# Routing the first batch's tokens inside the second batch's attention, and what the stage after attention then holds

## The chip, the core and the metric

One core of a Trainium2 chip (trn2). TensorE (PE) multiplies matrices, VectorE (DVE), ScalarE (ACT) and GpSimd (POOL) work on tiles, SyncE (SP) issues most DMAs. The metric is device time in microseconds of the one core.

## The reference, cut to what matters

Two sequences of 1024 tokens with 256 features go through one transformer layer: grouped attention (16 query heads, 4 key-value heads of 128, causal, rotary positions), layernorm, a mixture of experts, layernorm.

```
q = rope(x @ Wq.T); k = rope(x @ Wk.T); v = x @ Wv.T
x = layernorm(x + softmax(causal(q k^T / sqrt(128))) v @ Wo.T)
logits = x @ gate_w.T                      # (2048, 64)
topk_w, topk_ids = top_k(softmax(logits), 6);  topk_w /= sum(topk_w)
routed = sum over the 6 experts of  w * (silu(g) * u) @ w_down.T
shared = (silu(x @ sg.T) * (x @ su.T)) @ ws_down.T
x = layernorm(x + routed + shared)
```

## The kernel before, in words

There are three blocks of engine programs, one after the other: attention, routing (with the shared experts), experts. All engines meet at the end of a block.

**Attention** is software-pipelined in 4 rounds (k = 0 to 3) of 64 steps. A round takes two key-value heads of one batch, so batch 0 is done in rounds 0 and 1, batch 1 in rounds 2 and 3. A step is one tile of 128 queries of one head against its 1 to 8 tiles of 128 keys: of each 32 steps the first 16 have 1 to 4 key tiles (here the short half), the last 16 have 5 to 8 (the long half). The order on every engine is written out by the step number n: TensorE in step n forms the scores of n, transposes the probabilities of n-2, sums the output of the pair (n-4)/2, and does one fill of the projection bank proj_ps, if FILLS names one. Every product is three products of upper and lower parts (hi and lo, fp32r). FILLS: O (output projection of a pair) at steps 4m and 4m+1, Q at 4m+2, and at 4m+3 in turn T, K, V and nothing. K and Q are turned by the rotary tables: ScalarE copies the bank (taken), GpSimd multiplies by the cosine in two operations of 64 partitions that swap the halves (L347, L349), VectorE by the sine (turn_sin, L490), GpSimd adds (L353) and forms the lower part (L333). V comes as T, a product of 512 columns that is transposed later by 4 transposes (fill V, L585). VectorE takes the row maximum (neg_max, L508), the lower parts of probabilities (pt_lo, L468) and outputs (o_lo, L476) and adds the projected output to resid (L501). A fill waits (bank_free) until the one before it is taken out of the bank. Meanwhile SP writes SKIP rows into the buffer of expert rows in DRAM (rows_dram), 32 DMAs from 114 partitions, 8 rows each.

**Routing** takes all 16 tiles of 128 tokens together: statistics, square root on ScalarE, norm (L803), transposes to xt (L910), logits (L919), MAX8 and indices, masks of the six chosen experts (L816 to L821), counts and places by products with triangular and one matrices (L927 to L933), slot numbers (product, slots, slots_int, L854 to L856), then owner, triples (L858 to L865), the table of which expert each block of 256 rows has. ScalarE copies each token's row six times into rows (L768). GpSimd sends 96 indirect DMAs of 128 rows into rows_dram (L752). The shared experts run on TensorE (L942 gate-up, L956 and L957 down), 16 units in order, each of which needs a product by VectorE (hide, L875, L876) two units before it.

**Experts** walks over the blocks in triples; SP reads each block's expert from the table and loads rows (x_in) and weights.

Of the kernel before, what the change touches and what calls it, by code (L numbers as in the profile page):

```python
# [30 lines left out]
P = 128  # L31
B, S, H = 2, 1024, 256
T = B * S
# [20 lines left out]
LIST_BLOCKS = MAX_BLOCKS + 3  # L54
ROWS = LIST_BLOCKS * BLK
EMPTY_ROWS = 8
# [25 lines left out]
               key=lambda use: FILLS[use[0]][use[1]])  # L82
SPLIT_X = [-20, -4]
SPLIT_W = [-16, 16]
SPLIT_WO = [2, 34]

# [55 lines left out]

def runs(i, per, first, last):


    return i is not None and not (first and i < per) and not (last and i >= per)


def now(k, per, n):


    return (k + 1) * per + n

# [9 lines left out]
def attention(nc, dram, resid, consts):  # L163
    with ExitStack() as ctx:
# [24 lines left out]
        probs = sb("probs", [P, 4, S])  # L189
# [3 lines left out]
        ident = consts["ident"]  # L193

# [6 lines left out]
        x_in, w_in, wo_in, empty_out = sem("x_in"), sem("w_in"), sem("wo_in"), sem("empty_out")  # L201
# [5 lines left out]
        v_turning = sb("v_turning", [P, HALF])  # L207
# [7 lines left out]

        block = ctx.enter_context(nc.Block())
# [4 lines left out]
        def w_cols(kind, i):  # L221

            head = {"K": GROUP, "T": GROUP + 1}.get(kind, i % GROUP)
            return slice(head * HD, (head + 1) * HD)
# [15 lines left out]

        def lower_parts(eng, ops, k, n, first, last):

            i = at(SPLIT_X, n)
            if runs(i, SPLITS, first, last):
                cols = slice(i % 2 * HALF, (i % 2 + 1) * HALF)
                eng.wait_ge(x_hi_made, now(k, SPLITS, i + 1))
# [11 lines left out]
        def _(sp):  # L258
# [3 lines left out]
            def body(k, first, last):  # L262
                def batch_of(r):
                    return r % ROUNDS // (NKV // KV_ROUND)

# [4 lines left out]
                for n in range(FIRST, FIRST + STEPS):  # L270
                    i = at(SPLIT_X, n)
                    if runs(i, SPLITS, first, last):
                        sp.wait_ge(x_split, now(k, SPLITS, i))
                        sp.dma_start(x_raw[:], dram["xT"][bass.ds(batch_of(k + i // SPLITS), 1), i % 2]
                                     .rearrange("o p k t -> (o p) k t")).then_inc(x_in, 16)
# [10 lines left out]
                    if first and n == FIRST + STEPS - 1:  # L286
                        sp.dma_start(resid[:], dram["x"].rearrange("(i p) c -> p i c", p=P)).then_inc(resid_in, 16)
                        sp.wait_ge(consts_made, 2)
                    if not first and n % 8 == 0:
# [159 lines left out]
        def _(dve):  # L449
# [9 lines left out]
            def body(k, first, last):  # L459
# [60 lines left out]
                if first:  # L520
                    dve.wait_ge(resid_in, 16)
# [945 lines left out]
```

## Time and profile before

| | us |
|---|---|
| median of 3 runs | 1422.31 (1422.07 to 1423.52) |
| the profiled execution | 1425.77 |
| its span, first to last instruction | 1424.0 |
| attention | 0 to 884.1 |
| routing | 884.1 to 1077.2 |
| experts | 1077.2 to 1424.0 |

The profile records when each instruction ran on its engine and what it waited for. A busy TensorE is not TensorE at its peak. All times are from the start of the span.

### The profile page before, as it was taken

How to read it: one execution, taken by the hardware profiler on the slowest of the kernel's cores; microseconds unless marked ns; L12 is line 12 of the kernel's file. 1: busy time of each engine (PE TensorE's matmuls, PEld its weight loads, DVE VectorE, ACT ScalarE, POOL GpSimd, SP SyncE). 2: the span in 40 equal slices, each digit the busy share in tenths (PEclk: the TensorE clock that was granted, in tenths of full speed). 3: DMA queues.
4: the chain of work that ended last, by engine and by line, in shares of the span. 5: the costliest groups of instructions: out<-in, count | busy, mean ns of one | idle time of the engine just before them, and what ended most of it. 6: DMA issues, size and time to landing. Idle time of an engine off the chain costs nothing. (4 is left out here: it accounts for less than half of the span.)

```text
span 1424.0 us, 27954 instructions
## 1 busy us (share of the span) xinstructions
PE 1254.1 (88%) x8732; PEld 1117.1 (78%) x8732; DVE 991.5 (70%) x2012; ACT 846.5 (59%) x1875; POOL 809.8 (57%) x798
## 2 busy tenths in 40 slices
PE   3899999999999999999999997539925999999966
PEld 2789899899899899899899897536615999999954
DVE  2677677677677677777776777572204999999956
ACT  2666666566666566666665664622204989899932
POOL 4754754654754654754654630037774888888840
PEclk9999999999999999999999999559966999999979
DMA  6320040120040120140400001014225888888868
GB/s 224 116 76 1 11 153 23 57 76 1 21 151 15 57 76 1 27 150 11 122 1 2 1 1 34 1 49 104 104 101 172 263 260 262 257 263 263 267 204 269
DMA packets 100293, 151.29 MB, mean 106 GB/s; under 512 B 10410, under 2 KB 73038, under 8 KB 100196
## 3 DMA queue, kind: packets, MB, share of 16 engines
q1 hardware_dynamic: 89156, 124.75, 29.0%
q0 software_dynamic: 11040, 25.30, 5.3%
q8 instruction: 54, 0.88, 0.3%
q14 instruction: 43, 0.35, 0.1%
HBM read 92.51 MB, written 62.46 MB: 109 GB/s over the span
## 5 line engine op out<-in xcount | busy, mean ns | idle before, releaser
L508 DVE TENSOR_REDUCE neg_max<-scores 128x1 f32<-128x256 f32 (+7 forms) x256 | 192.6, 752 | 178.3 <-PE scores L611 178.1
L418 ACT ACTIVATE pt_hi<-pt 128x512 fp32r<-128x512 f32 (+3 forms) x384 | 174.8, 490 | 204.8 <-PE pt L620 201.7
L468 DVE TENSOR_TENSOR pt_lo<-pt,pt_hi 128x512 fp32r<-128x512 f32 (+3 forms) x384 | 200.8, 551 | 23.5 <-ACT pt_hi L418 21.6
L391 ACT ACTIVATE probs<-scores,neg_max 128x256 f32<-128x256 f32 (+7 forms) x256 | 190.1, 743 | 21.9 <-DVE neg_max L508 21.8
L539 PE MATMUL o_ps<-pt_hi,v_hi 128*128 128x256 f32 (+1 forms) x640 | 193.4, 302 | 4.9 <-DVE o_lo L476 4.8
L347 POOL TENSOR_TENSOR turned<-taken,cos 64x512 f32<-64x512 f32 x80 | 105.6, 1320 | 152.7 <-ACT taken L401 147.5
L540 PE MATMUL o_ps<-pt_lo,v_hi 128*128 128x256 f32 (+1 forms) x640 | 179.5, 281 | 0.0
L541 PE MATMUL o_ps<-pt_hi,v_lo 128*128 128x256 f32 (+1 forms) x640 | 179.1, 280 | 0.0
L620 PE MATMUL pt<-ident,probs 128*128 128x128 f32 x1152 | 168.2, 273 | 0.0
L1106 POOL DMA_INDIRECT results_dram<-y_sb,dest x134 | 145.2, 1083 | 32.8 <-issue 25.9
L611 PE MATMUL scores<-k_hi,q_lo 128*128 128x512 f32 (+4 forms) x384 | 151.5, 395 | 0.0
L333 POOL TENSOR_TENSOR q_lo<-turned,q_hi 128x512 fp32r<-128x512 f32 x64 | 82.6, 1291 | 113.9 <-ACT q_hi L428 113.9
L353 POOL TENSOR_TENSOR turned<-turned,turn_sin 128x512 f32<-128x512 f32 x80 | 103.8, 1298 | 72.7 <-DVE turn_sin L490 71.2
L752 POOL DMA_INDIRECT rows_dram<-rows,slots_int x96 | 94.2, 982 | 86.0 <-issue 86.0
L620 PEld LDWEIGHTS pt<-ident,probs 128*128 128x128 f32 x1152 | 134.9, 141 | 5.0
L606 PE MATMUL scores<-k_hi,q_hi 128*128 128x512 f32 (+4 forms) x384 | 132.1, 344 | 2.7 <-POOL q_lo L333 2.7
L607 PE MATMUL scores<-k_lo,q_hi 128*128 128x512 f32 (+4 forms) x384 | 131.1, 341 | 0.0
L539 PEld LDWEIGHTS o_ps<-pt_hi,v_hi 128*128 128x128 f32 x640 | 121.1, 189 | 10.2 <-issue 7.4
L540 PEld LDWEIGHTS o_ps<-pt_lo,v_hi 128*128 128x128 f32 x640 | 121.9, 191 | 0.0
L541 PEld LDWEIGHTS o_ps<-pt_hi,v_lo 128*128 128x128 f32 x640 | 121.2, 189 | 0.0
L501 DVE SCALAR_TENSOR_TENSOR resid<-proj_ps,row_inv,resid 128x256 f32<-128x256 f32 x256 | 110.7, 473 | 7.5 <-PE proj_ps L541 7.5
L349 POOL TENSOR_TENSOR turned<-taken,cos 64x512 f32<-64x512 f32 x80 | 105.8, 1323 | 6.3
(186 smaller groups left out, 3619.0 us busy)
## 6 DMA issues: line engine op xcount, KB each, us to landing
rows_dram<-empty SPq DMA_DIRECT2D x32, 919.1 KB
up_raw<-in_up SPq DMA_DIRECT2D x69, 368.0 KB, 3.9
x_in<-rows_dram SPq DMA_DIRECT2D x68, 258.0 KB, 3.5
parts<-results_dram SPq DMA_DIRECT2D x16, 768.0 KB, 9.8
down_raw<-in_down SPq DMA_DIRECT2D x69, 128.0 KB
down_raw<-in_down_tail SPq DMA_DIRECT2D x69, 112.0 KB
w_raw<-in_w SPq DMA_DIRECT2D x8, 768.0 KB, 9.1
x_raw<-in_xT SPq DMA_DIRECT2D x8, 512.0 KB, 5.0
```

What stands on the lines that cost most here:

```text
L391: nc.scalar.activation(probs[:, m % 4, 0:w], scores_ps[m % 2][:, score_cols(m)], ACT.Exp, bias=neg_max[:, m % 4:m % 4 + 1], accum_out=row_ ...
L418: nc.scalar.activation(pt_hi[m // 2 % 2][:, a:z, P * (m % 2):P * (m % 2) + P], pt_ps[c % 2][:, 0:P * (z - a)].rearrange("p (k q) -> p k q" ...
L468: nc.vector.tensor_tensor(pt_lo[m // 2 % 2][part], pt_ps[c % 2][:, 0:P * (z - a)].rearrange("p (k q) -> p k q", q=P), pt_hi[m // 2 % 2][pa ...
L508: nc.vector.tensor_reduce(neg_max[:, n % 4:n % 4 + 1], scores_ps[n % 2][:, score_cols(n)], AX.X, ALU.max, negate=True).then_inc(max_made, 1)
L539: nc.tensor.matmul(out, lh, rh, start=first, stop=False)
L540: nc.tensor.matmul(out, lh, rl, start=False, stop=False)
L541: return nc.tensor.matmul(out, ll, rh, start=False, stop=last)
L606: nc.tensor.matmul(out, q_hi[b][qt], k_hi[u][:, keys], start=True, stop=False)
L607: nc.tensor.matmul(out, q_hi[b][qt], k_lo[u][:, keys], start=False, stop=False)
L611: mm = nc.tensor.matmul(out, q_lo[b][qt], k_hi[u][:, keys], start=False, stop=True)
L620: mm = nc.tensor.transpose(pt_ps[c % 2][:, (t - a) * P:(t - a + 1) * P], probs[:, m % 4, t * P:(t + 1) * P], ident[:])
L1106: pool.indirect_dma_start(out=dram["results"], out_offset=bass.IndirectOffsetOnAxis(ap=dest[buf][:, s:s + 1], axis=0), in_=y_sb[buf][:, s, ...
```

## The change

The eight tiles of batch 0 (EARLY) are routed during the attention of batch 1, in two groups of four tiles (GT = 4, GROUPS = 4). Their VectorE operations are dealt over steps by the table EARLY_DVE, their transposes, logits and places are made by TensorE in the projection bank at steps 4m+3 (EARLY_TURN, EARLY_LOGITS, EARLY_PLACE), and their 48 sends go out two steps apart, in the end one step apart (EARLY_FILL), through a ring of four row buffers. For slots to be known before all counts are, each expert gets an area of 2048 rows in rows_dram; the block table then holds a row block for each block too, and SP reads it in the expert loop. The routing block does the other eight tiles (LATE); the counts move behind the slots, the shared experts' loops are written out. To make room in attention: V of rounds 2 and 3 is formed directly (no T), the rotary swap moves from GpSimd's cosine to VectorE's sine, x is split only once for each batch, probs has 2 buffers for 4, loads are issued 12 steps ahead. The clearing of rows_dram becomes 64 DMAs from 65 partitions, 32 rows each, one every four steps and never more than about 8 steps ahead of TensorE.

```diff
-LIST_BLOCKS = MAX_BLOCKS + 3
-ROWS = LIST_BLOCKS * BLK
-EMPTY_ROWS = 8
+CAP = T
+AREAS = E + 1
+ROWS = AREAS * CAP
+EMPTY_ROWS = 32
+EMPTY_DMAS = CAP // EMPTY_ROWS
+GT = 4
+GROUPS = TILES // GT
+EARLY = BT
+LATE = TILES - EARLY
+LOAD_AHEAD = 12
+EMPTY_EVERY = 4
+TURNED_V_ROUNDS = 2
+EARLY_DVE = {(1, 55): [(0, "stats", 0), (0, "stats", 1)], (1, 57): [(0, "stats", 2)], (1, 58): [(0, "stats", 3)],
...
+             (2, 31): [(0, "shift", 0), (1, "inverse", 0)], (2, 35): [(0, "weigh", 0)], (2, 39): [(0, "weigh", 1)],
+             (2, 43): [(0, "slot", 0)], (2, 47): [(0, "slot", 1)], (2, 50): [(0, "slot", 2)],
...
+             (3, 54): [(1, "slot", 8)], (3, 55): [(1, "slot", 9), (1, "slot", 10)], (3, 57): [(1, "slot", 11)]}
+EARLY_DEVIATION = {(1, 60): 0, (2, 20): 1}
+EARLY_EXP = {(2, 32): 0, (3, 28): 1}
+EARLY_TURN = {(2, 3): (0, 0), (2, 15): (0, 1), (2, 63): (1, 0), (3, 3): (1, 1)}
+EARLY_LOGITS = {(2, 19): 0, (3, 15): 1}
+EARLY_PLACE = {(2, 31): 0, (3, 31): 1}
+RING_ROWS = 4
+SENDS = EARLY * WAYS
+EARLY_FILL = {step: f for f, step in enumerate([2 * STEPS + 49 + 2 * f for f in range(SENDS // 2)]
+                                               + [3 * STEPS + 41 + 2 * f for f in range(GT)]
+                                               + [3 * STEPS + 48 + f for f in range(SENDS // 2 - GT)])}
...
@@ attention, SP
-                    if not first and n % 8 == 0:
-                        sp.dma_start(dram["empty"][bass.ds(k * 8 + (n // 8 - 1), 1)].rearrange("o p r c -> (o p) r c"),
-                                     empty[0:LIST_BLOCKS, :].unsqueeze(1).broadcast_to([LIST_BLOCKS, EMPTY_ROWS, ROW])).then_inc(empty_out, 16)
+                    if not first and step % EMPTY_EVERY == 0:
+                        c = (k * STEPS + step) // EMPTY_EVERY - FIRST // EMPTY_EVERY - 1
+                        sp.wait_ge(scored, now(k, STEPS, step - 8))
+                        sp.dma_start(dram["empty"][c], empty[0:AREAS, :].unsqueeze(1).broadcast_to([AREAS, EMPTY_ROWS, ROW])).then_inc(empty_out[c * GROUPS // EMPTY_DMAS], 16)
@@ attention, GpSimd
+            def send(f):
+                g, t, way = fill_of(f)
+                pool.wait_ge(rows_filled, f + 1)
+                pool.wait_ge(slots_made, g * TOPK + way + 1)
+                pool.wait_ge(empty_out[g], 16 * EMPTY_DMAS // GROUPS)
+                pool.indirect_dma_start(
+                    out=dram["rows"], out_offset=bass.IndirectOffsetOnAxis(ap=slots_int[:, t, way:way + 1], axis=0),
+                    in_=rows[:, f % RING_ROWS, :], in_offset=None, bounds_check=ROWS - 1,
+                    oob_is_err=False).then_inc(rows_sent[f % RING_ROWS], 16)
-                        nc.gpsimd.tensor_tensor(turned[r % 2][0:64], taken[r % 2][64:128], cos[64:128, pos], ALU.mult).then_inc(cos_made, 1)
-                        pool.wait_ge(cos_made, 2 * now(k, len(ROPES), r) + 1)
-                        nc.gpsimd.tensor_tensor(turned[r % 2][64:128], taken[r % 2][0:64], cos[0:64, pos], ALU.mult).then_inc(cos_made, 1)
+                        nc.gpsimd.tensor_tensor(turned[r % 2][:], taken[r % 2][:], cos[:, pos], ALU.mult).then_inc(cos_made, 1)
+                    if k * STEPS + n - 1 in EARLY_FILL:
+                        send(EARLY_FILL[k * STEPS + n - 1])
@@ attention, ScalarE, at the end of a step
+                    if k * STEPS + n in EARLY_FILL:
+                        f = EARLY_FILL[k * STEPS + n]
+                        g, t, way = fill_of(f)
+                        act.wait_ge(weights_made, g + 1)
+                        act.wait_ge(normed, GT * (g + 1))
+                        if f >= RING_ROWS:
+                            act.wait_ge(rows_sent[f % RING_ROWS], 16 * (f // RING_ROWS))
+                        nc.scalar.activation(rows[:, f % RING_ROWS, 0:H], resid[:, t, :], ACT.Copy)
+                        nc.scalar.activation(rows[:, f % RING_ROWS, H:ROW], goes_with[:, t, way, :],
+                                             ACT.Copy).then_inc(rows_filled, 1)
@@ attention, VectorE
+                nc.vector.tensor_tensor(turn_sin[r % 2][0:64], taken[r % 2][64:128], sin[64:128, pos], ALU.mult)
+                nc.vector.tensor_tensor(turn_sin[r % 2][64:128], taken[r % 2][0:64], sin[0:64, pos],
+                                        ALU.mult).then_inc(sin_made, 1)
...
+                    turn = fill_at(n - 2)
+                    if turn and turn[0] == "Q" and runs(turn[1], per("Q"), first, last):
+                        turn_by_sine(k, *turn)
...
+                    if turn and turn[0] == "K" and runs(turn[1], per("K"), first, last):
+                        turn_by_sine(k, *turn)
                     if runs(n, STEPS, first, last):
                         dve.wait_ge(scored, now(k, STEPS, n + 1))
                         nc.vector.tensor_reduce(neg_max[:, n % 4:n % 4 + 1], scores_ps[n % 2][:, score_cols(n)],
                                                 AX.X, ALU.max, negate=True).then_inc(max_made, 1)
+                    route(k, n)
@@ attention, TensorE
+                    if kind == "V":
+                        for t in range(4):
+                            tok = slice((4 * half(kind, i) + t) * P, (4 * half(kind, i) + t + 1) * P)
+                            for c in range(HK):
+                                mm = products(proj_ps[:, t * HD:(t + 1) * HD], (x_hi[:, c, tok], x_lo[:, c, tok]),
+                                              (w_hi[u][:, c, w_cols(kind, i)], w_lo[u][:, c, w_cols(kind, i)]), c == 0, c == HK - 1)
@@ routing, TensorE
             pe.wait_ge(shared_in, 48)
+            pe.wait_ge(xt_made, TILES // 2)
+            pe.wait_ge(mask_made, 1)
             gate_up(0, 0)
             gate_up(0, 1)
-            pe.wait_ge(slots_made, TOPK)
-            with pe.Fori(0, UNITS // 4 - 1) as q:
+            for q in range(UNITS // 4 - 1):
@@ experts, SP
-                sp.dma_start(x_in[buf][:], row_blocks[bass.ds(n, 1)].rearrange("o p s c -> (o p) s c")).then_inc(rows_in[buf], 16)
+                r = sp.value_load(table[0:1, bass.ds(P + n, 1)], min_val=0, max_val=ROWS // BLK - 1)
+                sp.dma_start(x_in[buf][:], row_blocks[bass.ds(r, 1)].rearrange("o p s c -> (o p) s c")).then_inc(rows_in[buf], 16)
```

## Rows read from the trace of the kernel before

**Rows 1.** Windows by stage: length, busy us (instructions) of each engine, PE clock, DMA share, GB/s.
```profile
34.00:884.10 850.10, 826.48 (x5860) 742.45 (x5860) 614.94 (x1182) 528.17 (x1230) 461.08 (x334) 1.00 0.16 49
884.10:1077.20 193.10, 111.20 (x568) 82.34 (x568) 70.08 (x191) 47.57 (x73) 96.83 (x107) 0.73 0.24 72
1077.20:1372.00 294.80, 270.62 (x2148) 259.57 (x2148) 266.18 (x541) 252.83 (x541) 238.74 (x341) 0.96 0.82 250
```

**Rows 2.** Timeline of VectorE in the routing stage: start, us, instruction, idle before.
```profile
891.44 5.26 DVE L803 TENSOR_SCALAR resid<-resid,moments,inv_dev 128x256 f32<-128x256 f32 x16
...
911.57 2.20 DVE L809 MAX8 top<-logits_ps 128x8 f32<-128x64 f32 x16 [14.88 <-PE logits_ps L919]
...
928.07 1.23 DVE L824 TENSOR_TENSOR shifted<-logits_ps,top 128x1024 f32<-128x1024 f32 x1 [0.15 <-DVE mask L821]
...
939.06 1.22 DVE L854 TENSOR_TENSOR product<-chosen,slot_of 128x1024 f32<-128x1024 bf16 x1
...
954.75 0.25 DVE L858 TENSOR_SCALAR started<-started,block_id 128x64 f32<-128x64 f32 x1
...
956.04 0.15 DVE L865 TENSOR_SCALAR triples_int<-triples_int 128x1 int32<-128x1 int32 x1
...
1041.22 0.69 DVE L884 TENSOR_TENSOR resid<-places_ps,resid 128x512 f32<-128x512 f32 x1 [4.33 <-PE places_ps L957]
```

**Rows 3.** Timeline of ScalarE in the routing stage.
```profile
910.18 17.95 ACT L768 ACTIVATE rows<-resid 128x1536 f32<-128x1536 f32 x13
928.15 1.28 ACT L772 ACT_TABLE_LOAD   x1
```

**Rows 4.** Timeline of GpSimd: the first two of 96 sends, and the last.
```profile
942.78 1.18 POOL L752 DMA_INDIRECT rows_dram<-rows,slots_int  x1 [57.06 <-issue]
944.26 0.98 POOL L752 DMA_INDIRECT rows_dram<-rows,slots_int  x1 [0.30 <-issue]
...
1064.98 0.98 POOL L752 DMA_INDIRECT rows_dram<-rows,slots_int  x1 [0.30 <-issue]
```

**Rows 5.** Instructions of the routing block's end (ns min/median/max; first start).
```profile
L654 POOLq DRAIN  x1: 7910/7910/7910, 1067.7 to 1067.7; - x1
```

**Rows 6.** Timeline of TensorE at the shared experts' start.
```profile
956.22 3.75 PE L942 MATMUL logits_ps<-xt,shared_up 128*128 128x256 f32 x8 [20.90 <-DVEq L868]
...
964.70 1.99 PE L942 MATMUL logits_ps<-xt,shared_up 128*128 x8 [0.56 <-DVE shared_hidden L876]
```

**Rows 7.** TensorE's waits from 50 to 880 us: total us, times, longest.
```profile
PE proj_ps L539 <- DVE v_lo L514: 10.4, 8, 1.3
PE proj_ps L539 <- DVE resid L501: 5.2, 8, 0.7
PE o_ps L539 <- DVE o_lo L476: 3.6, 16, 0.3
```

**Rows 8.** Timeline of TensorE in attention: products of 512 and of 128 columns.
```profile
521.38 0.40 PE L540 MATMUL proj_ps<-x_lo,w_hi 128*128 128x512 f32 x1
521.62 0.39 PE L541 MATMUL proj_ps<-x_hi,w_lo 128*128 128x512 f32 x1
...
525.81 0.28 PE L540 MATMUL o_ps<-pt_lo,v_hi 128*128 128x128 f32 x1
525.92 0.27 PE L541 MATMUL o_ps<-pt_hi,v_lo 128*128 128x128 f32 x1
```

**Rows 9.** The sine turn's line: ns min/median/max, first and last start.
```profile
L490 DVE TENSOR_TENSOR turn_sin<-taken,sin x80: 681/1022/1545, 20.3 to 843.4; 128x512 f32<-128x512 f32 x80
```

**Rows 10.** The same as rows 5, for the attention block's end.
```profile
L164 POOLq DRAIN  x1: 1409/1409/1409, 849.5 to 849.5; - x1
```

**Rows 11.** Windows of 10 us in attention, with and without clearing (columns as rows 1).
```profile
410.00:420.00 10.00, 10.00 (x72) 8.99 (x71) 6.57 (x11) 5.94 (x13) 3.72 (x3) 1.00 0.41 126
720.00:730.00 10.00, 10.00 (x77) 9.43 (x76) 8.44 (x16) 6.93 (x15) 3.42 (x4) 1.00 0.00 1
```

**Rows 12.** SP's own waits from 1100 to 1370 us.
```profile
SPq L1059 <- DVE down_lo L1269: 68.3, 63, 1.9
```

More of the change, by code:

```diff
@@ new lines, in early_at, with fill_of, early_bank @@
+def early_at(schedule, k, n):
+    for way_in in ((k, n), (k - 1, n + STEPS), (k + 1, n - STEPS)):
+        if way_in in schedule:
+            return schedule[way_in]
+    return None
+def fill_of(f):
+    g, way, t = f // (GT * WAYS), f // GT % WAYS, f % GT
+    return g, GT * g + t, way
+def early_bank(k, n):
+    for kind, uses in (("turn", EARLY_TURN), ("logits", EARLY_LOGITS), ("place", EARLY_PLACE)):
+        if early_at(uses, k, n) is not None:
+            return kind, early_at(uses, k, n)
+    return None
@@ L262, in body @@
             def body(k, first, last):
-                def batch_of(r):
-                    return r % ROUNDS // (NKV // KV_ROUND)
                 def kv_at(i):
                     return (k + i // SPLITS) % (NKV // KV_ROUND) * KV_ROUND + i % SPLITS
[L270 to L275, printed above, removed]
+                for step in range(FIRST, FIRST + STEPS):
+                    n = step + LOAD_AHEAD
+                    i = x_part(k, n, first, last)
+                    if i is not None:
+                        sp.wait_ge(x_split, SPLITS + i)
+                        sp.dma_start(x_raw[:], dram["xT"][i // SPLITS, i % 2]).then_inc(x_in, 16)
                     i = at(SPLIT_W, n)
@@ L544, in bank_free @@
                 def bank_free(n):
-                    for before in range(n - 1, 0, -1):
-                        use = fill_at(before)
-                        if use and (before < FIRST or runs(use[1], per(use[0]), first, last)):
+                    for earlier in range(n - 1, 0, -1):
+                        use = early_bank(k, earlier)
+                        if use:
+                            break
+                        use = fill_at(earlier)
+                        if use and use[0] == "T" and not turned_v(k, use[1]):
+                            continue
+                        if use and (earlier < FIRST or runs(use[1], per(use[0]), first, last)):
                             break
@@ L639, in body @@
                     use = fill_at(n)
-                    if use and runs(use[1], per(use[0]), first, last):
+                    if use and runs(use[1], per(use[0]), first, last) and (use[0] != "T" or turned_v(k, use[1])):
                         fill(n, *use)
+                    turn = early_at(EARLY_TURN, k, n)
+                    if turn is not None:
+                        bank_free(n)
+                        g, h = turn
+                        pe.wait_ge(normed, GT * g + 2 * h + 2)
+                        for t in range(2):
+                            for c in range(HK):
+                                mm = nc.tensor.transpose(proj_ps[:, (t * HK + c) * P:(t * HK + c + 1) * P],
+                                                         resid[:, GT * g + 2 * h + t, c * P:(c + 1) * P], ident[:])
+                        mm.then_inc(turned_x, 1)
@@ L774, in _ @@
             act.sem_inc(silu_made, 3)
-            with act.Fori(0, UNITS // 4) as q:
+            for q in range(UNITS // 4):
                 for u in range(4):
@@ L928, in _ @@
             mm.then_inc(places_made, 1)
-            for i in range(TILES):
+            for i in range(LATE):
                 out = places_ps[:, i * E:(i + 1) * E]
```

499 lines of the change are left out of this document (354 added, 145 removed).

## The prediction

> **What bounds the kernel.** I read the windows by stage first. Attention takes 850 us and TensorE is busy for 826 of them; the stage between attention and the experts takes 193.1 us with TensorE busy 111 and VectorE 70; the expert stage takes 295 us with VectorE and TensorE both above 90% [rows 1]. The 193 us stage is where no engine is full, so I read it engine by engine. VectorE first: layernorm, then a wait for the logits, top-6 and mask until 928.1, slot numbers from 939.1 to 954.8, the block table until 956.2 [rows 2]. ScalarE copies the rows to be sent, 13 tiles in 17.95 us, 1.38 us each, and loads a function table in 1.28 us [rows 3]. GpSimd starts its first send at 942.8; the second starts at 944.3 and the last of 96 at 1065.0, one every 1.284 us [rows 4]. The block then ends on GpSimd: its drain behind the sends lasts 7.9 us, to 1075.6 [rows 5]. TensorE starts the shared experts at 956.2, waits once for VectorE, runs from 964.7 without a gap [rows 6] and its last sum is added by 1041.9 [rows 2]. So the sends are last, 34 us behind the shared experts. From 50 to 880 us TensorE waits for somebody for only 19 us: 10.4 for v_lo, 5.2 for the addition into resid, 3.6 for o_lo [rows 7]. That stage is a full TensorE stream; anything added to it on TensorE is paid in full, and what is added elsewhere is paid where those waits grow.
>
> **The stage after attention, now for 8 of 16 tiles.** Its zero is its start, 884.1. Before, norm starts at 7.3 and the first max at 27.5, 20.1 us for 16 tiles [rows 2]. With half the stats norm starts at 4.3; two tiles must be normed before the first pair is turned (+0.7), and 8 tiles take half of 20.1, so the max starts at about 15.5 to 16. From max to mask was 16.5 us for 16 tiles [rows 2]; half is 8.3, and the two subtractions moved ahead add 0.8: mask at 25. On TensorE 44 mask products follow instead of 152, some 2 us, to 27. ScalarE has three more pairs to copy (to 19.5), then 8 tiles of rows at 1.38 and two exponentials with a table load, 11.0 + 2.1 [rows 3]: to 32.8. That is later than VectorE's weights (30), so the rows are ready at 33.2. Six slots at half of 15.7/6 us [rows 2] take 8.2, to 41.4. The table calculation, 7 operations in 1.44 us before [rows 2], is now some 19 in a row with the count of blocks in it: 4.0, to 45.5.
>
> The sends: the first at 33.2 + 1.4 + 1.1 = 35.7; 47 spacings and 1.2 for the last, 61.6; then landing and the drain of 7.9: 107.
>
> The shared experts: their first two units now run at 27 to 36, but the third needs the first product of VectorE, which is in order behind the table calculation: 46.6 on TensorE. From there to the last addition it took 964.70 to 1041.91, 77.2 us [rows 2, 6]. TensorE is idle for 10 us before; after its idle time before 956.2 the first eight gate-up products took 3.75 us where later ones take 1.99 [rows 6], 1.8 more, with their tail some 2.5, and I add that. End: 46.6 + 79.7 = 126.3, with VectorE's own drain 126.9. This is 20 us behind the sends: **the end moves from GpSimd to TensorE**. The stage ended at 1075.6 - 884.1 = 191.5, so the gain is 64.6 us, not the 84 that the sends alone would give. Unrolling the loop gives nothing: TensorE had no gap in it.
>
> **What attention pays.** (1) V of rounds 2 and 3 is formed directly. A 512-column product is issued 0.24 us after the one before it, a 128-column one after 0.11 [rows 8]. Removed per V: 6 x 0.24 + 4 x 0.1 = 1.8; added 24 x 0.11 = 2.65. Eight times +0.85 = +6.8. In the short half of each 32 steps TensorE stood 1.3 us behind v_lo; the longer product gives VectorE time, so four of these eight waits go: -5.2. (2) K's sine turn moves behind the addition into resid, the addition that TensorE waited for at K steps: -5.2 [rows 7]. (3) The sine turn is split in two operations of 64 partitions, and the swap leaves GpSimd, which has one product where it had two. One turn took 1.02 us in the median and 0.68 at least [rows 9], where GpSimd was quiet; two quiet ones are 1.36. I set this to 0, since GpSimd's second product, which ran beside the turn, is gone; if it isn't hidden it is 0.3 x 80 = 24 us of VectorE, a bound. The Trainium skill (SBUF — State Buffer, Who interferes with whom) says that a VectorE operation with two SBUF inputs contends with GpSimd's SBUF reads; the spread of the turn agrees, and by the rule the split costs less than twice the old mean. (4) TensorE's part of the early routing: four turns of 4 transposes (1.7), logits (2.4, an estimate: half of what 8 tiles of logits took in the stage after attention), 28 mask products (1.5): +5.6. (5) The projection bank: six early uses stand in front of an O fill and are taken late in the next step, by ScalarE or VectorE. By the wait of v_lo about 1 us each, +6; 0 to 12. (6) VectorE's insertions: 51 us for 16 tiles before (70.1 less 19 of shared work [rows 1]), so 26 for 8, about 35 in pieces of 256 columns. VectorE is busy 615 of 850 us [rows 1], so there is room; the price is lateness. Behind the insertion stand pt_lo, o_lo and the resid addition that TensorE needs. In the long half they have over a microsecond of slack, in the short half almost none: 12 short-half insertions at 0.3 to 0.5, the rest little: +6, bounds 0 and 35. (7) ScalarE: 48 fills of two copies, 0.6 us each, 28 us in all. Queued behind is o_hi, for which o_lo and the next output product wait. A dozen lie in the short half, at 0.4; the others at 0.1: +8, bounds 0 and 28. (8) Two square roots force a function table away and back, 4 loads of 1.28 [rows 3]: +3, bounds 0 and 5. (9) 4 of 8 x loads and their splits go, hidden before. The 48 sends on GpSimd take 1.3 us each; it is busy 461 of 850 us [rows 1] and loses 100 us of cosine products, so they are hidden, except at the end. The last fill comes some 6 us before the end of attention at the earliest, its send takes some 3.5 us to land, and then comes the drain: 7.9 us behind sends [rows 5] against 1.4 without them [rows 10]. Attention's block ends at 889 instead of 884: +5, bounds 0 and 9.
> Attention: 6.8 - 5.2 - 5.2 + 5.6 + 6 + 6 + 8 + 3 = +25, and +5 at its end.
>
> **The clearing of rows.** An area of 2048 rows for each expert makes the buffer 65 x 2048 rows of 1032 B, 137 MB; before, 30 MB were cleared. It goes out in 64 transfers of 2.15 MB, one in every 4 steps (13.2 us). The old ones moved 126 GB/s with a busy share of 0.41 of 16 engines [rows 11]: 6.6 engines. The source then had 114 partitions, and 6 is the largest number up to 16 that divides 114; for 65 it is 13. At 20 GB/s for an engine 13 give 260 GB/s, 8.3 us a transfer, and all is hidden; the expert stage shows that 250 GB/s can be had [rows 1]. TensorE was full with 126 GB/s beside it and with 1 [rows 11]. The other bound is 126 GB/s as before: 17 us a transfer. The Trainium skill (DMA: Bandwidth & Descriptors, Why a DMA increments its semaphore by 16 and not by 1) says that a transfer uses the largest number of engines up to 16 that divides the outermost size of both sides; the busy share agrees, and by the rule the clearing is hidden.
>
> **The expert stage.** Block counts are the same. SP reads one more value for each block, under 1 us. SP is queued behind down_lo for 68.3 us in 63 blocks, 1.1 each [rows 12]; the read takes that place. At the start it lies beside GpSimd's zeroing. 0.
>
> **Sum.** The profiled execution took 1425.8 (span 1424.0 and 1.8 around it), 3.5 over the median. 1425.8 - 64.6 + 25 + 5 = 1391; at the median's level 1387.6. I say 1387.
>
> **Rivals.** *A, as summed*, 0.62. *B, attention hides everything* (items 5 to 8 are 0, the rest about 2): 1422 - 65 + 5 = 1363. For it: VectorE idle 28%, ScalarE 38%. Against: short-half waits of rows 7. 0.10. *C, every inserted operation is paid in full*: 35 + 28 + 5.6 + 12 + 5, with the split turn 24: +110 - 65: 1467, slower. It decides from +65 us in attention, half a microsecond in each of 128 steps. 0.07. *D, the clearing keeps 126 GB/s*: 137.4 MB take 1090 us; the block can't end before 1110 to 1120, 230 late, and the total is 1422 - 65 + 230 = 1587. It decides below 162 GB/s for the stretch of 850 us, and turns the sign below some 150. Rows 11 alone speak for it, the share against. 0.08. *E, the shared experts don't wait for the table calculation*, so the sends end the stage at 107 or the shared experts at 113: 14 to 20 us more gain, 1370. 0.05. *F, the change moves work but late routing is held by something else new* (the table's trip, rows), gain near zero: 0.02. The rest, 0.06, is A with an attention cost of 45 to 65.
> Faster 0.82, within 0.2% (what a measurement of this kernel can tell from no change) 0.02, slower 0.16. The range takes in B and A with attention at up to +55: 1360 to 1415.
>
> **What would show it.** The windows: attention 25 to 35 longer, at TensorE near 97% busy; the next stage 127 long instead of 191.5. The chain in it: GpSimd's 48 sends end some 20 us before TensorE's last down product; the third shared unit starts right after the last table operation. GpSimd's drain at attention's end is near 8 us and ends it. The clearing shows a DMA share near 0.8 for 60% of the time. TensorE's waits in the short halves of rounds 2 and 3 name ScalarE and VectorE. Wrong would be: an attention stage over 900 with DMA busy to its end (D), or TensorE's waits above 60 us (C).

## The result and the profile after

The changed kernel takes 1416.9 us in the median of 20 runs (1409.4 to 1421.9), the kernel before 1424.2 (1422.1 to 1426.1, 20 runs): 0.9948 of before, 95% interval 0.9936 to 0.9959. It is faster by 7 us. I had forecast 1387 against the 1422.3 known then, 35 us less; 1416.9 lies 2 us above my range.

The profiled execution of the changed kernel took 1411.4 us with a span of 1409.6. Windows by stage, columns as in [rows 1]:

```profile
34.00:934.00 900.00, 850.49 (x6040) 761.43 (x6040) 693.68 (x1398) 553.23 (x1328) 391.14 (x297) 0.99 0.66 169
934.00:1066.00 132.00, 100.16 (x428) 71.34 (x428) 49.62 (x148) 30.88 (x54) 48.49 (x54) 0.82 0.21 57
1066.00:1372.00 306.00, 278.49 (x2181) 267.14 (x2182) 268.07 (x557) 251.80 (x541) 240.81 (x343) 0.95 0.83 255
```

Against [rows 1] attention ends 50.2 us later (934.3 against 884.1), the routing stage lasts 131.6 us where it lasted 192.0 (-60.4), and what follows 343.7 where it was 347.9 (-4.2). The sum is -14.4 us, the difference of the two spans. That is twice the difference of the medians, because this execution is one of the changed kernel's quickest: in two later profiles of the same kernel (spans 1419.0 and 1418.3) attention took as long within 2 us and the routing stage within 1, but the experts took 350.6 and 350.4 us.

The routing stage came out nearly as forecast. GpSimd's last sends before the stage and the last in it:

```profile
926.02 0.98 POOL L445 DMA_INDIRECT rows_dram<-early_rows,early_slots_int  x1 [0.30 <-issue]
927.30 0.98 POOL L445 DMA_INDIRECT rows_dram<-early_rows,early_slots_int  x1 [0.30 <-issue]
...
968.95 1.01 POOL L1055 DMA_INDIRECT rows_dram<-rows,slots_int  x1 [33.83 <-DVE slots_int L1153]
...
1029.86 0.98 POOL L1055 DMA_INDIRECT rows_dram<-rows,slots_int  x1 [0.30 <-issue]
1065.87 0.53 POOL L1442 MEMSET hidden<- 128x512 f32 x1 [35.03 <-POOLq L957]
```

The first send starts 34.7 us into the stage (forecast 35.7); the last is issued 34 us before VectorE's last addition, and GpSimd then waits 35 us for the block's end. So the end has moved from GpSimd [rows 4, 5] to TensorE. VectorE, at the end of the block table and at the first shared unit, and the last addition:

```profile
979.46 0.15 DVE L1175 CAST triples_int<-triples 128x1 int32<-128x1 f32 x1
979.65 0.15 DVE L1176 TENSOR_SCALAR triples_int<-triples_int 128x1 int32<-128x1 int32 x1
986.00 0.42 DVE L1186 TENSOR_TENSOR shared_hidden<-shared_silu,logits_ps 128x256 f32<-128x256 f32 x1 [6.20 <-ACT shared_silu L1087]
...
1064.29 0.69 DVE L1195 TENSOR_TENSOR resid<-shared_y,resid 128x512 f32<-128x512 f32 x1 [4.33 <-PE shared_y L1271]
```

TensorE in the same stretch:

```profile
979.83 3.75 PE L1256 MATMUL logits_ps<-xt,shared_up 128*128 128x256 f32 x8 [16.89 <-DVEq L1179]
```

TensorE stood for 16.9 us and started its first shared unit when the table was done, 45.6 us into the stage. (A unit is one shared expert's gate and up products for 256 tokens; L1179 is the line where VectorE first releases hidden_made.) The table took from 975.6 to 979.8, 4.2 us (forecast 4.0).

In attention, TensorE's waits from 50 to 880 us, in answer to [rows 7]:

```profile
PE o_ps L789 <- DVE o_lo L728: 20.0, 24, 2.0
PE proj_ps L789 <- DVE v_lo L756: 7.5, 8, 1.5
PE pt L889 <- DVE pt_lo L720: 4.4, 6, 1.1
PE proj_ps L789 <- ACT x_raw L575: 3.6, 4, 2.1
PE proj_ps L789 <- ACT v_turning L583: 3.3, 2, 1.9
PE proj_ps L789 <- DVE resid L748: 2.1, 8, 0.4
PE proj_ps L789 <- DVE base L630: 1.2, 2, 0.7
```

They are 42 us where they were 19, and TensorE's busy time grew by 24, some of it at the lower clock (last section). The wait for o_lo, 3.6 us in 16 places before, is 20.0 us in 24.

From the start of each step's row maximum on VectorE, which stands in every step, one gets the length of 16 steps. The table has attention's 16 groups of 16 in order (two for each half round, the short scores first), each from its first row maximum to that of the next group, the last one to that of step 255:

```
before        40.2 61.4 44.5 61.4 | 44.5 61.4 44.5 61.4 | 44.5 61.4 44.5 61.4 | 44.5 61.4 44.5 52.2
changed       41.6 62.4 46.7 62.4 | 46.7 62.4 46.8 64.0 | 46.2 72.4 47.4 64.8 | 48.6 67.9 48.3 55.0
```

The bars stand between rounds. In the first two rounds the early routing does not yet run, bar a few statistics, and still every group of short scores costs 2.2 us more (the first 1.4) and every group of long ones 1.0. This price repeats to 0.1 us, so it belongs to something in every step. From group 8 on the direct V (below, 0.9 in a long group) and the routing's own price come on top, above all in one group, 72.4.

### The profile page after: what moved, and what is told of

Same layout as the page of the kernel before. It is cut to its first block and busy times, and to the rows that moved or that the text cites. A ratio compares the mean times of both kernels' runs of the same rounds, so it can differ in the third digit from the quotient of the medians.

```text
span 1409.6 us, 28399 instructions
## 1 busy us (share of the span) xinstructions
PE 1264.9 (90%) x8780; PEld 1125.1 (80%) x8780; DVE 1051.0 (75%) x2191; ACT 854.4 (61%) x1956; POOL 694.4 (49%) x718
## 5 line engine op out<-in xcount | busy, mean ns | idle before, releaser
L466 POOL TENSOR_TENSOR turned<-taken,cos 128x512 f32<-128x512 f32 x80 | 104.1, 1301 | 144.9 <-ACT taken L519 144.7
L1422 POOL DMA_INDIRECT results_dram<-y_sb,dest x134 | 148.6, 1109 | 33.7 <-issue 27.3
L789 PE MATMUL proj_ps<-wo_hi,o_hi 128*128 128x256 f32 x256 | 78.0, 305 | 18.9 <-DVE v_lo L756 7.5
L789 PE MATMUL proj_ps<-x_hi,w_hi 128*128 128x512 f32 x176 | 73.6, 418 | 16.5 <-DVE w_lo L356 12.4
## 6 DMA issues: line engine op xcount, KB each, us to landing
wo_raw<-in_wo SPq DMA_DIRECT2D x8, 512.0 KB, 19.4
```

Of the source, the lines that this page charges most:

```text
L789: nc.tensor.matmul(out, lh, rh, start=first, stop=False)
L1422: pool.indirect_dma_start(out=dram["results"], out_offset=bass.IndirectOffsetOnAxis(ap=dest[buf][:, s:s + 1], axis=0), in_=y_sb[buf][:, s, ...
```

## Experiments

Runs beginning with b are the kernel before with one part of the change; those with a are the changed kernel with one part altered. Ratios are against the kernel before on the same chip. This matters: on two of the chips before took 1494 us (last section), on the others 1423 to 1424. The edits are shown shortened, with words for long code.

**The swap of halves alone (b_swap).**

```diff
-  gpsimd: turned[0:64] = taken[64:128] * cos[64:128];  turned[64:128] = taken[0:64] * cos[0:64]
+  gpsimd: turned[:] = taken[:] * cos[:]
-  vector: turn_sin[:] = taken[:] * sin[:]
+  vector: turn_sin[0:64] = taken[64:128] * sin[64:128];  turn_sin[64:128] = taken[0:64] * sin[0:64]
```

> The kernel before with one part of the change: the swap of halves moves from GpSimd's cosine products to VectorE's sine products, so a turn has two sine products of 64 partitions and one cosine product of 128. Theory 1 (half of the 50 us that attention grew by belongs to changes that act in every step, and the split turn is the largest of them): 8 to 20 us slower. Rival (the split is hidden, as I predicted: the 25 us come from elsewhere): within 3 us of before.

1532.9 us against 1494.2, ratio 1.0253 (1.0232 to 1.0273): 38.7 us slower, near twice the most that I expected. VectorE's groups of instructions from 35 to 900 us (count, then busy us and mean ns), first of b_swap:

```profile
L489 DVE TENSOR_TENSOR turn_sin<-taken,sin 64x512 f32<-64x512 f32 x77 | 60.6, 787 | 1.1
L488 DVE TENSOR_TENSOR turn_sin<-taken,sin 64x512 f32<-64x512 f32 x77 | 56.5, 734 | 2.4
```

and of b_order, below, which has the whole product:

```profile
L465 DVE TENSOR_TENSOR turn_sin<-taken,sin 128x512 f32<-128x512 f32 x77 | 75.9, 985 | 0.1
```

117 us where one product takes 76. The quick ones show it best: min and median are 686 and 687 ns for 64 partitions, and 681 is the least for 128 [rows 9]. Half the partitions take VectorE as long as all of them, 0.69 us against 0.68. The Trainium skill (VectorE: DVE Perf Modes, Why `tensor_reduce` can't reduce along partition axis) says that each of the 128 partition lanes is a pipeline of its own; the trace agrees.

Where it is paid, TensorE's waits from 50 to 880 us in b_swap, against [rows 7]:

```profile
PE proj_ps L539 <- DVE resid L501: 21.3, 16, 2.5
PE proj_ps L539 <- DVE v_lo L514: 16.8, 15, 1.7
PE o_ps L539 <- DVE o_lo L474: 2.2, 10, 0.2
```

They are 40.3 us where they were 19.2.

**VectorE's order alone (b_order)**: the row maximum behind v_lo and K's sine product, K's sine product behind the addition into resid.

```diff
-  recip; sine product (K or Q); add into resid; row maximum; v_lo
+  sine product (Q); recip; add into resid; v_lo; sine product (K); row maximum
```

> The kernel before with VectorE's order in a step as in the changed kernel: the row maximum comes behind v_lo and behind K's sine product, and K's sine product behind the addition into resid. I predicted 5.2 us of gain from it. Theory 1: it gains no more than 3 us, or loses up to 5, since the row maximum is now late for the exponential. Rival: the gain of 5 us is there and another part pays more than the trace suggests.

1494.2 us, ratio 1.0005 (0.9994 to 1.0016). Nothing. TensorE's waits from 50 to 880 us:

```profile
PE o_ps L544 <- DVE o_lo L484: 12.5, 24, 1.1
PE proj_ps L544 <- DVE v_lo L512: 5.9, 8, 0.7
PE proj_ps L544 <- DVE resid L504: 1.0, 1, 1.0
```

The wait for resid fell from 5.2 to 1.0 us, nearly as priced, and that for v_lo from 10.4 to 5.9, and the wait for o_lo rose from 3.6 to 12.5. The sum is 19.4 as it was 19.2: the lateness only changed its name.

**Swap and order together (b_order_swap)**, the two diffs above.

> The kernel before with the swap on VectorE and VectorE's order in a step as changed. The swap alone cost 39 us, the order alone 0. Theory (the order is there to let TensorE's two waits, for v_lo and for the addition into resid, come ahead of the longer sine products): together they cost 22 to 28 us, which is what the changed kernel's attention lost in rounds without early routing. Rival (they add up): 36 to 42 us.

1448.8 us against 1423.1, ratio 1.0175 (1.0158 to 1.0192): 25.7 us, inside the 22 to 28. Its groups of steps are 41.8 62.4 47.0 62.4 | 47.0 62.4 47.0 62.4 and so on: the price in the changed kernel's first rounds, to 0.3 us. So the order is worth 13 us once the sine product is split (11 by the length of all steps, 870.4 against 859.6 us; b_swap ran on one of the slower chips), and nothing before. TensorE's waits:

```profile
PE o_ps L544 <- DVE o_lo L484: 19.9, 23, 2.1
PE proj_ps L544 <- DVE v_lo L512: 11.7, 8, 1.5
PE proj_ps L544 <- DVE resid L504: 1.3, 8, 0.2
```

They are 32.9 us, 13.7 more than before. The rest of the price is the clock: seven stretches of about 3.4 us at half clock in attention, where before has none, lose 11.9 us by my estimate (half of their length). Together 25.6, where the steps took 25.7 us longer. In b_swap the same sum is 21.1 of waits and half of nine such stretches, 15.3: 36.4, where the steps took 36.5 longer.

**Two buffers of probabilities (b_probs2)**

```diff
-  probs = sb("probs", [P, 4, S])
+  probs = sb("probs", [P, 2, S])
-  act.wait_ge(transposed, now(k, CHUNKS, chunks_before(m - 3)))
+  act.wait_ge(transposed, now(k, CHUNKS, chunks_before(m - 1)))
```

> The kernel before with two buffers of probabilities in place of four, so ScalarE's exponential of a step waits until TensorE has transposed the probabilities of two steps earlier. Theory: this is the part of the change that nothing in my sum accounts for, 5 to 15 us slower. Rival: the exponential comes later than that transpose anyway; within 2 us of before.

1494.8 us, ratio 1.0001 (0.999 to 1.0013), every group of steps as before. The rival holds.

**The clearing (b_clear64)**

```diff
-  if not first and n % 8 == 0: clear 8 rows of each of 114 blocks
+  if not first and n % 4 == 0: clear 32 rows of each of 65 areas of 2048
```

> The kernel before with the changed kernel's clearing alone: a buffer of 65 times 2048 rows, cleared in 64 transfers of 2.15 MB from 65 partitions, one in every four steps, where 32 transfers of 0.94 MB were. The blocks read the same few rows. Theory: the clearing is hidden, within 3 us of before. Rival 1 (the traffic slows the cores' work or makes the chip grant a lower clock: the clock fell to 0.97 or 0.98 in the first five stretches of the changed kernel's attention): 8 to 15 us slower and the same dips in the granted clock. Rival 2: it is the spread between runs, 12 us wide after and 4 us before, that comes with the clearing.

1493.8 us, ratio 1.0002 (0.9989 to 1.0014). It is hidden, with a DMA share of 0.70 to 0.76 up to 820 us, and the granted clock stays at 1.00 from 140 us on. So the clock's dips are not the traffic's, and neither is the spread (1491.6 to 1498.7, before beside it 1491.4 to 1497.2).

**V formed directly in the last two rounds (b_vdirect)**

```diff
+  if kind == "V" and not turned_v(k, i): 24 products of 128 columns into proj_ps
```

> The kernel before with V of the last two rounds formed directly, and nothing else. I priced it at 6.8 us of TensorE less 5.2 of the waits for v_lo that it covers, +1.6. Theory: 0 to +3 us. Rival: the waits stay and the products are added to them, +6 to +9; or more is covered, -3.

1429.1 us against 1424.3, ratio 1.0028 (1.0018 to 1.0038): +4.8 us, between my theory and the rival. TensorE is busy 7.7 us longer (834.2 against 826.5), where I had priced 6.8; the waits for v_lo fell only from 10.4 to 6.4, where I had priced 5.2, and those for resid and o_lo stayed (5.0 and 3.4 us). The last 1 us stands in gaps too short to be listed as waits. By groups it is 0.9 us in each long one and 0.3 in each short one from group 8 on.

**The changed kernel again (a_again, a_again2)**

> The changed kernel unchanged, as the base for the three beside it and because this chip need not be the one of the first measurement: on the chip of the first four experiments the kernel before took 1494 us instead of 1424, with the shared experts' TensorE waiting for its next instruction while the sends ran. Every theory: if this is a chip of the first kind, 0.995 of before; on one of the second kind the result depends on whether the 48 sends that are left hold the instructions up as 96 did, and could be 0.95 to 1.00.

> The changed kernel once more, as base for the two beside it. On a chip of the first kind 0.995 of before. On one of the second kind (before 1494 us) the two near relatives of it that ran there took 1468 and 1469, so 0.980 to 0.985 is expected: the shared experts' wait for instructions beside the sends shrinks with the number of sends.

1417.7 us, 0.995 (0.9931 to 0.9968), and 1415.6, 0.9931 (0.9914 to 0.9947). The same as at first.

**The swap back on GpSimd where it can be (a_mixed)**: not everywhere. In the kernel before, GpSimd waits for all of its own earlier results before the two swapping products; with sends among them that would be their landings. What that would cost was not measured.

```diff
+  def swaps_on_vector(k, kind, i): return k + i // per(kind) >= ROUNDS - 1
+  where it is false: GpSimd's two cosine products and VectorE's one sine product, as before
-  EARLY_FILL starts at 2 * STEPS + 49
+  EARLY_FILL starts at 2 * STEPS + 57
```

> The changed kernel with the swap of halves back on GpSimd (two cosine products of 64 partitions, one sine product of 128) for the first three rounds' heads; the last round's stay as changed, since GpSimd's sends are under way then, and the first batch's 24 first sends start 8 steps later for the same reason. Theory 1 (the split sine product is most of what attention pays): three quarters of the turns lose 0.5 us of VectorE each, attention gets 20 to 30 us shorter, total 0.975 to 0.985 of before on a chip of the first kind. Rival (the early routing is what costs, the swap is worth 39 us only in the old order): 0 to 8 us.

1408.7 us, ratio 0.9879 (0.985 to 0.9908), 8.9 us less than a_again, where I expected 20 to 30. The groups tell where: 40.2 61.4 44.5 61.4 | 44.5 61.4 44.6 63.5 | 46.3 70.6 47.0 64.7 | 48.6 69.5 51.7 55.0. Until the early routing starts the steps are those of before, 11 us less than changed: the price of the first two rounds is the swap's, and nothing else's. From group 8 to 12 undoing the swap gives only 3 us, and the groups of the last round, where the swap stays on VectorE, cost 5 more. My reading, not tested by itself: the 5 are the sends, now later and in fewer steps, and beside the routing VectorE and ScalarE are late anyway, so that the half microsecond of a sine product is not what is waited for.

**The shared experts ahead of the block table (a_hide)**

```diff
+  VectorE's first release of hidden_made and added, which stood behind the table, goes ahead of all
   for j in range(TOPK):
       product, slots, slots_int of way j
+      if j in (2, 3): hide(0, j - 2)
-  the block table's 19 operations in a row; then hide(0, 0), hide(0, 1)
+  five of the table's operations behind each pair of shared units
```

> The changed kernel with VectorE's order after the routing changed: the shared experts' first products stand between the slot operations, and the block table's 19 operations are spread over the first shared units, so TensorE waits for neither. In the changed kernel's trace its first shared unit started 45.7 us into the stage, when the table was done. Theory (the end of the stage is TensorE's chain behind the table): shared units start at 28 to 30, and the end comes 12 to 17 us earlier, where the sends' drain (107 us predicted, the last send was issued 29 us before the end) or TensorE (115) ends it; total 10 to 17 us less than the changed kernel. Rival: the sends' landing ends it just behind, gain under 5 us.

1403.4 us, ratio 0.9858 (0.9842 to 0.9875), 14.3 us less than a_again. TensorE's first unit starts at 962.8, 28.7 us into the stage; the third waits once for VectorE's first products, and no later unit waits:

```profile
972.39 3.78 PE L1283 MATMUL logits_ps<-xt,shared_up 128*128 128x256 f32 x8 [3.46 <-DVE shared_hidden L1158]
```

The stage lasts 119.1 us instead of 131.6, and still ends with TensorE: the last send is issued at 1030.7, VectorE's last addition at 1051.6.

**Smaller areas, less clearing (a_cap512)**

```diff
-  CAP = T;  EMPTY_EVERY = 4
+  CAP = 512;  EMPTY_EVERY = 16
```

> The changed kernel with areas of 512 rows for each expert instead of 2048, which hold this input's rows: the buffer is 34 MB, the clearing 16 transfers of 2.15 MB, one in 16 steps. Clearing alone cost the kernel before nothing. Theory: attention keeps its 901 to 903 us and its dips of the granted clock, total within 3 us of the changed kernel (0.993 to 0.997 of before). Rival: the clearing together with the longer loads of weights and the sends holds something up in the changed kernel; 5 us or more less. Open on the side: the changed kernel's runs spread over 12 us, before's over 4, and between two profiles the expert stage alone differed by 7 (343.7 and 350.5); if areas spread over 137 MB do that, the spread is gone here.

1468.7 us against 1493.6, ratio 0.982 (0.9775 to 0.9866), on a chip where the changed kernel itself was not run. By the trace: groups of steps 41.5 62.4 46.7 62.4 | 46.7 62.4 46.7 64.0 | 46.2 72.4 47.4 64.8, the same as changed to 0.1 us, up to the last, which took 58.4 us. Its runs spread from 1462.4 to 1475.1, so the wide areas don't make the spread. Whether the total is within 3 us of the changed kernel this chip can't tell.

**ScalarE's order (a_reorder)**. In the worst group TensorE waits for the bank of the first turn. ScalarE in the changed kernel:

```profile
512.33 1.48 ACT L557 ACTIVATE w_hi<-w_raw 128x1536 fp32r<-128x1536 f32 x1
513.70 0.59 ACT L575 ACTIVATE x_raw<-proj_ps 128x512 f32<-128x512 f32 x1
...
530.61 1.28 ACT L568 ACT_TABLE_LOAD   x1
531.90 0.20 ACT L568 ACTIVATE early_deviation<-early_deviation 128x4 f32<-128x4 f32 x1
532.02 0.37 ACT L583 ACTIVATE v_turning<-proj_ps 128x256 f32<-128x256 f32 x1
```

and TensorE, which does nothing else meanwhile:

```profile
514.34 0.53 PE L789 MATMUL proj_ps<-wo_hi,o_hi 128*128 128x256 f32 x1 [2.09 <-ACT x_raw L575]
...
532.43 0.39 PE L789 MATMUL proj_ps<-wo_hi,o_hi 128*128 128x256 f32 x1 [1.46 <-ACT v_turning L583]
```

```diff
+  early turn copy, early logits copy
   x_hi, w_hi, wo_hi copies; square root
-  early turn copy, early logits copy
```

> The changed kernel with ScalarE's order in a step changed: its copies of the early routing's products out of the projection bank (four turns, two logits) stand ahead of the copy of w and of the square root with its table load. In the trace TensorE waited for them 3.6 and 3.3 us in six places, the longest 2.1 behind the 1.48 us copy of w and 1.5 and 1.9 behind the table load, and the first of these was followed by 3.6 us at half clock. Theory: those waits go and with them the clock's dip behind the first, 4 to 8 us less than the changed kernel. Rival: what was behind them is late in another place, 0 to 2.

1468.0 us, ratio 0.9814 (0.9787 to 0.984). The waits went (3.6 and 3.3 us to 2.2 and 0.5), the group fell from 72.4 to 68.0, and that of the next round from 67.9 to 66.5. But the ones behind them rose, 47.4 to 49.0 and 48.3 to 49.4, and the last took 60.0. Attention as a whole, from first row maximum to the block's end, is 903 us as in the changed kernel (901 to 903), and the total is that of a_cap512 beside it. No gain is shown, as the rival says; but the first fifteen groups are 3 us shorter, and the last, which took 55.0 to 58.4 us in other runs with a ring of four rows, hides that here.

**A ring of three rows (a_ring3)**

```diff
-  RING_ROWS = 4
+  RING_ROWS = 3
```

> The changed kernel with a ring of three rows for the early sends where there are four, so that ScalarE's fill of a row waits for the landing of the send three before it. In four profiles ScalarE waited 5.2 to 15.2 us for such landings in the last 60 us of attention, and the last 16 steps took between 55.0 and 60.0 us with them where before had 52.2. Theory (that wait is paid by attention, and its variation is part of the spread between runs): 4 to 12 us more than the changed kernel, with a spread at least as wide. Rival (the fills are off the path): within 1.5 us.

1428.7 us, ratio 1.003 (1.0014 to 1.0046): 13.1 us more than a_again2 beside it, just above the 4 to 12 expected and enough to undo the change. In the two profiles the last 16 steps took 66.7 us for 57.2, and no other group differs by more than 0.2. ScalarE, in its own waits from 600 to 938 us, first of a_again2 and then of a_ring3:

```profile
ACT early_rows L597 <- DMA rows_dram<-early_rows,early_slots_int: 8.2, 4, 3.1
```

```profile
ACT early_rows L597 <- DMA rows_dram<-early_rows,early_slots_int: 15.5, 4, 6.0
```

So a fill that waits for a send to land is on attention's path: everything ScalarE owes TensorE stands behind it.

**Three repairs together (a_best, a_best_again)**: a_mixed, a_hide and a_reorder.

> The changed kernel with three repairs together: the swap on GpSimd for the first three rounds' heads (worth 9 us alone), the shared experts ahead of the block table (worth 14 alone), ScalarE's order as in the run beside it. Theory: they act in different places and add up: 0.973 to 0.980 of before, 25 to 31 us less than the changed kernel. Rival: the reordering and the swap repair the same lateness, so 20 to 24.

> The changed kernel with its three repairs again, for its profile and time beside the changed kernel on the same chip. On a chip of the first kind 1386 to 1392 us, 0.974 to 0.978 of before; on one of the second kind 0.967 again, with the changed kernel at 0.98 to 0.985.

On the slower chip 1444.2 us, ratio 0.9674 (0.9649 to 0.9698). Beside a_again2 it took 1390.7 against 1415.6, ratio 0.9774 (0.9748 to 0.9799) to before: 24.9 us less than the changed kernel, where the swap and the shared experts gave 8.9 and 14.3 alone. That leaves 1.7 us for the third repair, within the spread of the runs. This version beats both kernels.

## Why the prediction was wrong

I forecast attention and its end at +30 us; it took +50. I forecast the next stage at -64.6; it was -60.4. The experts, which I had at 0, were -4.2 in the profiled execution, and the level of the runs is the rest. The outcome is the one to which I gave 0.06, A with a dearer attention.

**The step that failed is (3), the split sine product, set to 0.** I named 24 us as its bound and took the other end, "since GpSimd's second product, which ran beside the turn, is gone". Alone it cost 25.7 us (b_order_swap). No wait of TensorE names GpSimd, in [rows 7] or after. They name VectorE: two operations of 0.69 us stand where one of 0.69 to 1.6 stood, with o_lo queued behind them in the short steps. I argued with VectorE's mean load, idle 28%, where the waits of [rows 7] said that in the short halves it had nothing to spare. That 24 comes so near is luck: it counted VectorE's busy time, while the price is lateness and clock, and in the old order the same split cost 38.7. In the changed kernel itself 11 us of it are shown, in the first two rounds (a_mixed).

**Step (2), -5.2 for K's sine product behind the addition, was 0.** The wait that I took away came back under the name o_lo (b_order). It pays only together with the split.

**Step (1), V direct, +1.6, was +4.8.** The products cost 7.7 us for 6.8, and the waits gave back 4.0 for 5.2.

**Steps (4) to (8), +28.6, were some 22.** That is what is left of 52.3 (33.2 to 934.3 less 35.3 to 884.1) after 25.7 and 4.8. It is a remainder, and it takes the swap to cost as much beside the routing as alone; a_mixed suggests that it costs less there, and then these items cost more. None of them was measured by itself. Of its places the runs name three: waits for the bank behind w_hi and the table load (a_reorder takes 4.4 us out of the worst group, and later ones give most of it back), fills that wait for landings (in the last group, which is 2.8 to 7.8 us longer than before), VectorE's pieces ahead of pt_lo and o_lo. My item (7) priced the fills' busy time; a_ring3 shows that ScalarE also pays the wait for the DMA in front of them, which I had not seen. What the busy time itself costs was not measured. At attention's end I gave 5 us; the distance from the last row maximum to the next block grew from 14.9 to 17.3, 2.4: GpSimd's drain behind the early sends lasted 4.0 us, not the 7.9 of [rows 5].

**The stage after attention: 131.6 for 126.9.** "Their first two units now run at 27 to 36" is the failed step. The diff moves the wait on slots_made away, but gate_up also waits for hidden_made, which VectorE releases only behind the table. [rows 6] had said so: the wait of 20.9 us there ends on L868, the line of that release, not on slots_made. So TensorE began the first unit, not the third, at 45.6, and the third at 53.6 for 46.6. From there to the end it took 77.1 us, not 79.7, since the slow start that I had added fell on the first unit. Rival E is the repair of just this, and a_hide shows its worth, 12.5 us of stage.

**Rival D, the clearing**, is refuted (b_clear64), though attention did end past 900 us, my sign for it. The DMA share in attention was 0.66; from 227 to 237 us, one transfer, it was 0.74 to 0.81, which is 13 of 16 engines as computed, at 180 to 210 GB/s where I had taken 260. **The expert stage** is unchanged within its own spread. **The level**: I took it that a profiled execution lies 3.5 us over the median as before's did. The changed kernel's runs spread over 12 us, and its first profile lay 5.5 us under the median. Two parts of the spread are seen: the last 16 steps, 55.0, 57.3 and 57.2 us in its three profiles (55.0 to 60.0 in all nine with a ring of four rows), and the experts, 344 or 350. In the quicker expert stage TensorE's weight loads waited 12.1 us for an instruction at y_ps, in the slower ones 22.3 and 20.5, before 21.0. What chooses between them was not found.

## What to carry to other kernels

When TensorE's stream is full, look at which engine it waits for in the tightest steps, and price an edit on that engine there: an operation that is cut in two by partitions cost VectorE double here, and its mean idle share says nothing. A wait that is taken away should be followed to the next one in the queue before it is booked as a gain. A new transfer whose buffer is reused makes the engine that fills it wait for a landing, and all that the engine owes others stands behind that wait.

## What the hardware showed beside this

**A long stall can be paid nearly twice.** In the changed kernel o_lo was late at 165 us. VectorE before it:

```profile
161.38 1.38 DVE L707 TENSOR_TENSOR turn_sin<-taken,sin 64x512 f32<-64x512 f32 x1
162.77 0.69 DVE L708 TENSOR_TENSOR turn_sin<-taken,sin 64x512 f32<-64x512 f32 x1
163.48 0.42 DVE L764 TENSOR_REDUCE neg_max<-scores 128x1 f32<-128x256 f32 x1
163.82 0.68 DVE L720 TENSOR_TENSOR pt_lo<-pt,pt_hi 128x512 fp32r<-128x512 f32 x1
164.42 0.41 DVE L728 TENSOR_TENSOR o_lo<-o_ps,o_hi 128x256 fp32r<-128x256 f32 x1
```

TensorE, and its windows (the granted clock is the third number from the end):

```profile
164.98 0.36 PE L789 MATMUL o_ps<-pt_hi,v_hi 128*128 128x256 f32 x1 [1.81 <-DVE o_lo L728]
```

```profile
165.00:166.00 1.00, 1.00 (x7) 0.97 (x8) 1.00 (x4) 0.59 (x1) 1.00 (x1) 1.00 0.77 182
166.00:167.00 1.00, 1.00 (x4) 0.82 (x3) 0.28 (x2) 0.67 (x2) 1.00 (x2) 0.63 0.73 173
167.00:168.00 1.00, 1.00 (x4) 0.73 (x3) 0.00 (x0) 0.00 (x0) 0.34 (x1) 0.50 0.58 148
168.00:169.00 1.00, 1.00 (x5) 0.48 (x3) 0.00 (x0) 0.60 (x1) 0.16 (x1) 0.50 0.32 87
169.00:170.00 1.00, 1.00 (x6) 0.82 (x6) 0.31 (x1) 0.02 (x1) 1.00 (x1) 0.66 0.20 71
170.00:171.00 1.00, 1.00 (x12) 1.00 (x10) 0.80 (x2) 0.74 (x3) 0.13 (x1) 1.00 0.40 124
```

After a wait of 1.81 us TensorE had its full clock for a microsecond, and then for about 3.4 us the lower of its two, 1.2 GHz, which lost it another 1.7 us (an estimate, half of 3.4). A stretch like it began near the waits of 1.8 us at 274 and 383 and of 2.1 at 514, but none near six other waits of 1.8 to 2.0 us, at 57, 494, 614, 726, 748 and 843. What decides is not known. Attention before had no such stretch. With swap and order alone there are seven, and each window of some 110 us from 140 us on has a clock of 0.98 or 0.99; with the order alone it is 1.00.

**A half of the partitions is no half of the work** (b_swap above).

**The chip matters.** On two chips, with the kernel before at 1494 us, attention took the same time to 0.1 us in each group, and the shared experts did not. TensorE there in b_order, while the sends run:

```profile
1027.24 0.58 PE L947 MATMUL logits_ps<-xt,shared_up 128*128 x1 [2.21 <-issue]
1030.05 0.58 PE L947 MATMUL logits_ps<-xt,shared_up 128*128 x1 [2.21 <-issue]
1032.85 0.58 PE L947 MATMUL xt_ps<-xt,shared_up 128*112 x1 [2.21 <-issue]
```

Before most single products it waits 2.2 us, for nothing that the profile names, until the sends are through, and the stage lasts 260.6 us instead of 192.0. With half of the sends there it lasted 171.4 (a_cap512, against 131.6 in the changed kernel elsewhere). So on such a chip the change is worth more: its two near relatives ran at 0.981 and 0.982 of before. The expert stage was longer too on the chip where these ran, 360 to 363 us in three profiles against 344 to 351 for the changed kernel and its variants elsewhere; why is not known. That the products wait for their instructions, whose transfers the sends hold up, is my reading and was not tested.
